# State space layers: step sizes summed from three terms by TensorE, positive part added by VectorE, one slot sooner; two input terms of a unit on GpSimd

## What is computed

```python
x_in, z = split(layernorm(x) @ in_w.T)
xc  = silu(causal_conv(x_in) + cb)
dtr, Bm, Cm = split(xc @ xp_w.T)                # 8, 16 and 16 wide
dt  = softplus(dtr @ dt_w.T + dt_b)             # the step sizes
def step(h, (dt_t, B_t, C_t, u_t)):
    h = h * exp(dt_t * A) + (dt_t * u_t) * B_t  # decay, input term
    y = sum_n(h * C_t)
y = (scan(step) + xc * D) * silu(z)
x = y @ out_w.T + x
```

## Time and profile before

| | us |
|---|---|
| median of 3 runs | 2846.63 (2842.55 to 2849.23) |
| profiled execution: device time | 2842.8 |
| its span, first to last instruction | 2840.9 |
| part of the span in the state space units (first scan to last gated y) | 562.5 to 1463 |
| its mean granted TensorE clock | 0.944 of full |

### The profile page before, as it was taken

One profiled execution on the slowest core, in us unless ns is written; L12 is line 12 of the kernel. 1 busy time (PEld: TensorE's weight loads), 2 busy tenths in 40 slices (PEclk: granted clock), 3 DMA queues, 4 the chain that ended last, 5 costly groups with the idle time before them and its releaser, 6 DMA issues. The chain is left out here.

```text
span 2840.9 us, 37719 instructions
## 1 busy us (share of the span) xinstructions
PE 2448.3 (86%) x10998; PEld 1399.6 (49%) x10998; DVE 1979.1 (70%) x3955; ACT 1695.2 (60%) x3534; POOL 1150.7 (41%) x951
## 2 busy tenths in 40 slices
PE   7999978388898989898878899968878998799977
PEld 5766644244454444454433344445553444555555
DVE  6888755499999999999965444355644444577754
ACT  3555523398988888989943244347753443466643
POOL 1000010399999999999950000032210001254432
PEclk9999979699999999999989999989998998999998
DMA  2000033134343434344433211100002110000000
GB/s 102 1 1 1 1 109 64 60 147 153 148 155 144 153 146 152 146 152 147 164 144 76 76 60 60 60 1 1 0 1 88 77 60 27 1 1 0 0 0 16
DMA packets 34611, 205.53 MB, mean 72 GB/s; under 512 B 4000, under 2 KB 5152, under 8 KB 13216
## 3 DMA queue, kind: packets, MB, share of 16 engines
q1 hardware_dynamic: 34464, 203.83, 20.0%
HBM read 201.19 MB, written 2.62 MB: 72 GB/s over the span
## 5 line engine op out<-in xcount | busy, mean ns | idle before, releaser
L1266 POOL TENSOR_TENSOR mam_state_c<-mam_state,weights_r 128x1024 f32<-128x1024 f32 x256 | 599.5, 2360 | 67.6 <-DVE mam_state L1214 66.9
L1214 DVE TENSOR_TENSOR_SCAN mam_state<-banks,mam_dbu 128x1024 f32<-128x1024 f32 x256 | 579.8, 2275 | 5.2 <-ACT banks L1342 4.1
L1425 PE MATMUL banks<-mam_state_c,identity 128*128 128x512 f32 x1024 | 507.1, 633 | 9.9 <-POOL mam_state_c L1266 9.4
L1342 ACT ACTIVATE banks<-mam_dt,mam_a_neg 128x255 f32<-128x255 f32 x1024 | 423.8, 461 | 47.7 <-DVE mam_state L1214 45.6
L1425 PEld LDWEIGHTS banks<-mam_state_c,identity 128*128 128x128 f32 x1024 | 196.7, 202 | 230.6 <-issue 184.9
L1192 DVE TENSOR_TENSOR mam_dbu<-banks,weights_r 128x1024 f32<-128x1024 f32 x224 | 266.9, 1203 | 9.9 <-ACT banks L1350 9.9
L424 ACT ACTIVATE at_probs<-banks,at_nmax 128x256 f32<-128x256 f32 x256 | 118.0, 473 | 137.7 <-DVE at_nmax L365 137.7
L2386 POOL TENSOR_TENSOR at_attention<-at_relu 128x512 f32<-128x512 f32 x128 | 131.1, 1043 | 124.3 <-ACT at_relu L2430 82.8
L896 DVE TENSOR_TENSOR m2a_hidden<-m2a_gelu,m2a_comb_spread 128x512 f32<-128x512 f32 x120 | 80.7, 690 | 116.4 <-ACT m2a_gelu L923 113.8
L896 DVE TENSOR_TENSOR m2b_hidden<-m2b_gelu,m2b_comb_spread 128x512 f32<-128x512 f32 x120 | 80.7, 690 | 116.5 <-ACT m2b_gelu L923 114.0
L923 ACT ACTIVATE m2b_gelu<-banks,weights_r 128x512 f32<-128x512 f32 x128 | 85.2, 686 | 101.7 <-PE banks L943 101.6
(11 more groups left out here) (520 smaller groups left out, 5132.9 us busy)
## 6 DMA issues: line engine op xcount, KB each, us to landing
weights_r<-mam_bc_rows SPq DMA_DIRECT2D x128, 1024.0 KB, 4.6
m2a_comb_spread<-m2a_comb_rows SPq DMA_DIRECT2D x15, 1024.0 KB, 7.1
m2b_comb_spread<-m2b_comb_rows SPq DMA_DIRECT2D x15, 1024.0 KB, 8.3
m1a_comb_spread<-m1a_comb_rows SPq DMA_DIRECT2D x14, 512.0 KB, 7.1
m1b_comb_spread<-m1b_comb_rows SPq DMA_DIRECT2D x14, 512.0 KB, 7.2
weights_r<-in_mb SPq DMA_DIRECT2D x1, 4332.0 KB, 13.0
weights_r<-in_m SPq DMA_DIRECT2D x1, 4200.0 KB, 13.8
weights_r<-in_a SPq DMA_DIRECT2D x1, 2632.0 KB, 13.1
```

The source lines that it names most:

```text
L1214: dve.tensor_tensor_scan(flat2(h[:, i % 4, :, :, :]), decay(i), flat2(dbu[:, i % 4, :, :, :]), 0.0, ALU.mult, ALU.add).then_inc(h_ready, 1)
L1266: pool.tensor_tensor(hc[:, j % 4, :, :, :], h[:, j % 4, :, :, :], c_rows(j), ALU.mult).then_inc(hc_ready, 1)
L1342: i = act.activation(decay(j)[:, o + 1:o + S], dt[:, q, c, 1:S], ACT.Exp, scale=aneg[:, l, k:k + 1])
L1425: k = pe.matmul(y_bank(q)[:, :], K.ident[:, :], flat(hc[:, j % 4, n, :, :]), start=(j == 0 and n == 0), stop=(j == NP - 1 and n == 1))
```

## The change

- The rows copy moves from slot 1 to slot 0 on ScalarE, the dt product from slot 2 to slot 1 on TensorE (still ahead of the slot's sum), Abs and Exp from slot 2 to slot 1. The +1 stays in slot 2; the -1 becomes 1 - (1 + e), and a Relu of v from PSUM follows it on ScalarE, in slot 2.
- In slot 4, after its sum, TensorE adds e, 1 - (1 + e) and ln(1 + e) into bank 7 by three matmuls with the identity, waiting for Ln ahead of the third.
- In slot 4, after the scan, VectorE adds Relu(v) to the bank and writes dt, in place of the step L1183.
- GpSimd loses L1230 and L1251 and gains a second input term of a unit: slots 3 and 6, issued in slots 1 and 4. VectorE has 6 of them left instead of 7.
- The layer norm transposes of `after` wait for dt instead of the correction.

```diff
-    BY_POOL = (4,)
+    BY_POOL = (3, 6)
@@ vector, prepare
                     if nxt and i == 4:
-                        dve.wait_ge(rounding_ready, b + 1)
-                        dve.scalar_tensor_tensor(flat(vw[:, :, :]), K.ps[7][:, :], 0.0, flat(vw[:, :, :]), ALU.max,
-                                                 ALU.subtract).then_inc(vw_ready, 1)
+                        dve.wait_ge(dt_sum, b + 1)
+                        dve.wait_ge(relu_ready, b + 1)
+                        dve.tensor_tensor(flat(dt[:, q, :, :]), K.ps[7][:, :], flat(vw[:, :, :]), ALU.add).then_inc(dt_ready, 1)
@@ gpsimd
-                def rounding(i, nxt):
-                    if nxt and i == 4:
-                        pool.wait_ge(part_ready, b + 1)
-                        pool.tensor_tensor(vw[:, :, :], va[:, :, :], ve[:, :, :], ALU.subtract).then_inc(rounding_ready, 1)
                     if nxt and i == 5:
-                        pool.wait_ge(ln_ready, b + 1)
-                        pool.wait_ge(vw_ready, b + 1)
-                        pool.tensor_tensor(dt[:, q, :, :], vl[:, :, :], vw[:, :, :], ALU.add).then_inc(dt_ready, 1)
                         pool.wait_ge(dt_ready, b + 1)
                         pool.tensor_tensor(du[:, q, :, :], dt[:, q, :, :], xc[:, q, :, :], ALU.mult).then_inc(dus_ready, 1)
@@ scalar, prepare
-                    if nxt and i == 1:
+                    if nxt and i == 0:
                         act.wait_ge(bc_ps, b + 1)
                         ...
                         act.activation(rows[0:40, :], K.ps[7][0:40, 0:S], ACT.Copy).then_inc(rows_ready, 1)
-                    if nxt and i == 2:
+                    if nxt and i == 1:
                         act.wait_ge(dt_ps, b + 1)
                         act.activation(flat(va[:, :, :]), K.ps[7][:, :], ACT.Abs).then_inc(abs_ready, 1)
                         act.wait_ge(abs_ready, b + 1)
                         act.activation(ve[:, :, :], va[:, :, :], ACT.Exp, scale=-1.0).then_inc(exp_ready, 1)
+                    if nxt and i == 2:
                         ...
-                        act.activation(va[:, :, :], vu[:, :, :], ACT.Identity, bias=K.neg_one[:, 0:1]).then_inc(part_ready, 1)
+                        act.activation(va[:, :, :], vu[:, :, :], ACT.Identity, bias=K.ones[:, 0:1],
+                                       scale=-1.0).then_inc(part_ready, 1)
+                        act.activation(flat(vw[:, :, :]), K.ps[7][:, :], ACT.Relu).then_inc(relu_ready, 1)
@@ tensor, prepare
-                    if nxt and i == 2:
+                    if nxt and i == 1:
                         pe.wait_ge(rows_ready, b + 1)
                         ...
                     if after and i == 5:
                         if nxt:
-                            pe.wait_ge(vw_ready, a)
+                            pe.wait_ge(dt_ready, a)
                         norm_tensor(K, N, pe, a, K.ps[7])
+                def step_sizes(i, nxt):
+                    if nxt and i == 4:
+                        pe.wait_ge(part_ready, b + 1)
+                        pe.wait_ge(relu_ready, b + 1)
+                        pe.matmul(K.ps[7][:, :], K.ident[:, :], flat(ve[:, :, :]), start=True, stop=False)
+                        pe.matmul(K.ps[7][:, :], K.ident[:, :], flat(va[:, :, :]), start=False, stop=False)
+                        pe.wait_ge(ln_ready, b + 1)
+                        pe.matmul(K.ps[7][:, :], K.ident[:, :], flat(vl[:, :, :]), start=False, stop=True).then_inc(dt_sum, 1)
@@ tensor, slot: prepare, the sum of slot i-2, then
+                    step_sizes(i, nxt)
```

More of the change, by code:

```diff
@@ L1015, in stage_state_space @@
         vu = sb(f"{tag}_dt_one_plus", [P, C, S])
-        vw = sb(f"{tag}_dt_correction", [P, C, S])
+        vw = sb(f"{tag}_dt_relu", [P, C, S])
         dbu = sb(f"{tag}_dbu", [P, 4, 2, C, S])
@@ L1102, in state_space_layers @@
         (dve_s, act_s, dve_hold, xn_ready, xin_ps, z_ps, xc_ready, z_ready, bc_ps, rows_ready, rows_out, dt_ps,
-         abs_ready, exp_ready, ln_ready, plus_ready, part_ready, rounding_ready, bias_ready, mean_ready, vw_ready, dt_ready, dup_ready, dus_ready, da_ready, dbu_dve, dbu_pool,
+         abs_ready, exp_ready, ln_ready, plus_ready, part_ready, relu_ready, dt_sum, bias_ready, mean_ready, dt_ready, dup_ready, dus_ready, da_ready, dbu_dve, dbu_pool,
          h_ready, hc_ready, sum_done, yg_ready, out_ps, done) = make_sems(
@@ L1106, in state_space_layers @@
                     "bc_product rows_ready rows_written dt_product abs_ready exp_ready ln_ready "
-                    "one_plus_ready one_plus_less_one rounding_ready ln_bias minus_mean correction_ready dt_ready dtu_in_bank dtu_ready decay_ready dbu_by_vector "
+                    "one_plus_ready one_less_one_plus relu_ready dt_sum ln_bias minus_mean dt_ready dtu_in_bank dtu_ready decay_ready dbu_by_vector "
                     "dbu_by_pool state_ready state_c_ready sum_issued y_gated_ready out_product unit_done")
@@ L1180, in prepare @@
                     if nxt and i == 4:
-                        b = nxt[1] + nxt[0] * B
-                        dve.wait_ge(rounding_ready, b + 1)
-                        dve.scalar_tensor_tensor(flat(vw[:, :, :]), K.ps[7][:, :], 0.0, flat(vw[:, :, :]), ALU.max,
-                                                 ALU.subtract).then_inc(vw_ready, 1)
+                        l, s, q = nxt
+                        b = s + l * B
+                        dve.wait_ge(dt_sum, b + 1)
+                        dve.wait_ge(relu_ready, b + 1)
+                        dve.tensor_tensor(flat(dt[:, q, :, :]), K.ps[7][:, :], flat(vw[:, :, :]), ALU.add).then_inc(dt_ready, 1)
                 def input_term(u, j):
@@ L1255, in slot @@
                 def slot(i, now, last, nxt, after):
-                    rounding(i, nxt)
                     at = lagged(i, 1, NP, now, last)
@@ L1278, in slot @@
                     prepare(i, nxt, after)
[L1280 to L1284, removed]
+                before_units(prepare)
                 over_units(pool, slot, 1)
@@ L1413, in prepare @@
                         k.then_inc(xin_ps, 1)
+                def step_sizes(i, nxt):
+                    if nxt and i == 4:
+                        b = nxt[1] + nxt[0] * B
+                        pe.wait_ge(part_ready, b + 1)
[4 more added lines that the diff above has]
+                        pe.matmul(K.ps[7][:, :], K.ident[:, :], flat(vl[:, :, :]), start=False, stop=True).then_inc(dt_sum, 1)
                 def slot(i, now, last, nxt, after):
@@ L1444, in slot, with prepare_all @@
                         k.then_inc(out_ps, 1)
-                before_units(prepare)
+                def prepare_all(i, nxt, after):
+                    prepare(i, nxt, after)
+                    step_sizes(i, nxt)
+                before_units(prepare_all)
                 over_units(pe, slot, 3)
```

## The result

| | before | changed |
|---|---|---|
| median of 4 runs, us | 2846.8 | 2813.3 (2811.5 to 2816.7) |
| ratio | | 0.9885, 95% interval 0.9871 to 0.9898 |
| span of the profiled execution, us | 2840.9 | 2809.6 |
| a unit, us (30 units) | 28.15 | 27.05 |

33 us less. The windows between starts of the gated y (now L1200) answer to the earlier trace rows: all 30 units, the first 23 of them, the last 7. Columns: window, its length, busy time of TensorE, its weight loads, VectorE, ScalarE, GpSimd, granted clock, DMA share, GB/s.

What follows compares the result with a forecast made beforehand. VectorE's queue (27.4 us a unit) plus 0.6 us from TensorE's clock bound it. Units save 27.0 us, ends gain 2.2 and lose 2.3: net 26.9, 2842.8 to 2815.9; plus 3.8 for the median, 2820; range 2797 to 2842.

Steps and rivals of the forecast that it cites:

- The clock: TensorE, slot 5: three matmuls fill idle time, the clock stays at 2.4 GHz, 0.6 us a unit gained.
- VectorE's input term: VectorE: one input term of 1.13 us less a unit, of which about 0.4 us remain as gain.
- The chain: Scan 6 end to next: decays, rows copy, dt product, last sum, then VectorE from the gated y; 27.2 us a unit.
- scan 2 with the statistics: VectorE, in the chain behind the gated y: scan with layer norm statistics, taken as 3.05 us.
- The second check: Slot 4: the sum of three beats VectorE's add by 0.25 us; in the last layer the add waits 0.2 us.
- GpSimd's product of pair 2: GpSimd: state times C of pair 2 ends 0.1 us before TensorE asks for it.
- Waits of TensorE: TensorE idle about 1 us for the layer norm in slot 5 and under 1 us for the rows.
- The ends: Unit 0 and the last unit gain 2.2 us together; the path ahead of unit 0 loses 2.3 us.
- VectorE alone: Rival: the chain is shorter and VectorE's queue bounds; 26.4 us a unit, 2794 us; chance 0.10.
- The clock rival: Rival: remaining waits let TensorE's clock fall and it becomes the bound; 26 us slower, 2872 us; chance 0.12.
- No table load came with the Relu: Rival: ScalarE's Relu needs two more table loads of 1.28 us each; 28.3 us a unit, 2851 us; chance 0.03.

Runs made afterwards that it cites:

- e3: Kernel before plus three zero-weight matmuls in slot 4 on TensorE, where the changed kernel has the sum of three; 2829.0 us, ratio 0.9935.
- e5: Changed kernel with TensorE's gate product of slot 5 ahead of the layer norm transposes; 2817.4 us, ratio 0.9886.
- e12: Changed kernel with only the sum of three moved ahead of slot 4's state sum on TensorE; 2809.0 us, ratio 0.9869.
- e4: Changed kernel with the dt product of slot 1 behind the last sum on TensorE instead of ahead of it; 2853.8 us, ratio 1.002.
- e9: Changed kernel with ScalarE's rows copy of slot 0 between the two halves of the second decays; 2811.7 us, ratio 0.9867.
- e10: e9 with TensorE's gate product ahead of the layer norm transposes as well; 2809.1 us, ratio 0.9859.
- e2: Changed kernel with one input term on GpSimd (slot 4) as before, step sizes as changed; 2881.7 us, ratio 1.012.
- e11: e10 with the sum of three ahead of slot 4's state sum on TensorE; 2795.2 us, ratio 0.9821.
- e1: Kernel before with two input terms on GpSimd (slots 3 and 6 instead of 4), step sizes as they were; 2864.8 us, ratio 1.0056.
- e6: Changed kernel with ScalarE's rows copy of slot 0 ahead of the second decays instead of behind them; 2850.2 us, ratio 1.0001.

## Why the prediction was right

The sign, the size and the mechanism held: 2820 predicted, 2813.3 measured, 26.9 us less against 31.3 in the profiled execution. Part of that closeness is luck. The 30 units gave 32.9 us where 27.0 were forecast, and 2.1 us of scatter in the later blocks brought the total nearer.

- *The clock.* Expected back at 1.00 and worth 0.6 us a unit, the larger part of the gain. It is at 1.00, and e3 gives it alone 18 of 33 us, 28.15 to 27.59 over the 30 units. One reading behind it was off: the 23.1 us of waits before the gated y in the earlier trace rows hold 4.7 of the last unit, which have nothing to do with the clock; 18.4 in 22 units is the figure.
- *VectorE's input term.* Expected to bring 0.4 us of its 1.13, the rest going into a new wait. It brought 27.57 - 27.02 = 0.55 against the full-clock unit, and 0.60 against the mean of e3's first 23 units.
- *The chain.* Worked out as 10.75 + 16.45 = 27.2. Measured from the first decays' release to the gated y 10.7, from there to the end of scan 6 16.3 (1082.10 to 1098.36). The term that was mis-sized is scan 2 with the statistics: 3.05 in the earlier trace rows contained a gap of about 0.2; now it is 2.86. In other units of the kernel before the same stretch took 2.86 (from 569.12) and 3.30 (from 597.26), so 3.05 was the figure of one unit; no run shows what makes the gap. That is 4.2 us in 23 units. Another 1.7 came from the last seven: the last interval has nothing prepared beside it and took 26.4, and the first of them was still 27.02. e5 and e12 show that neither TensorE's queue nor the sum of three sets the unit, e4, e9 and e10 that shortening the chain takes the wait before the gated y away.
- *The second check.* Margin 0.25 expected, 0.15 found; GpSimd's product of pair 2 was to end 0.1 us before TensorE asks for it, and does (1087.44 and 1087.54); 0.2 us of wait in the last layer expected and found (0.21 at 1254.59). e2 and e10 show how near that row is: 1.03 and 0.65 us as soon as GpSimd comes later or the rest sooner.
- *Waits of TensorE.* About 1 us ahead of the layer norm transposes and under 1 us for the rows: 0.93 and 0.25. What ends the first is the add, at 1092.85; the layer norm, which the prediction named, ends at 1092.70.
- *The ends.* Wrong in three terms that nearly cancel. Ahead of unit 0, 2.3 us were to be lost; the add is 3.0 us later (551.95 against 548.94 of the earlier trace rows), 0.7 more than forecast, as the three matmuls ran at a granted clock of 0.60. But behind them the convolution runs at a clock of 1.00, where it ran at 0.72 in the kernel before. It starts 1.3 us later and takes 3.67 instead of 4.97, and the first scan starts at the same time. Unit 0 was to gain 1.1 and lost 0.3: the clock was 0.50 at its start, a sum took 3.75 us, and the add waited 1.33 us where its forerunner had waited 0.69. The last unit gained 0.7 of 1.1.
- *The rivals.* VectorE alone did not bound, since the wait of 0.82 stood in its way; with that chain and the sum of three moved, e11 comes near it. The clock rival didn't occur, but in e4 it shows in nine of 30 units after one reordering. No table load came with the Relu. GpSimd as the bound is what e1 shows when its step-size work stays.

## What to carry over

When an engine runs its queue in order, ask of each moved instruction what it waits for and who stands behind it: the sum of that loop, taken from start-to-start distances, gave the unit to 0.2 us, while the busy sums alone gave 26.3. When all engines are busy 94% to 97%, a removed wait is worth little until the next margin of 0.1 to 0.3 us is moved too: e9, e10 and e11 are three steps for 18 us, and the first two together gave 4. And before giving TensorE more work, look at where it idles; work in the right gap can pay for itself.

## Not expected of the hardware

- TensorE's clock does not follow from the length of the wait ahead. In the kernel before it held through 2.89 us of idle time in three units, and fell behind the same 2.89 us at 690.44 (0.58 in the four us behind) and behind 3.13. In e4 23 units have a wait of 2.2 to 2.3 us; behind nine of them it fell (0.57 in the four us behind), behind 14 it did not, as behind the 2.30 us at 980.72, and all have the same instructions ahead. What decides between them was not settled.
- The table load before the first decays' Exp ran at 1075.71 in the changed kernel, while TensorE computed the B, C and rows product. With a copy that brings no table load put ahead of that Exp (e6), the load came behind the copy and its wait for TensorE, and its 1.28 us, which had been hidden, came into the open.
